# Decoder layer: cross-attention queries and keys projected turned, float32 scores on 32-row strips in pairs of heads

## The reference, cut to what matters

```python
x = _layernorm(x + _L0_attn_ref(x, ...))            # self attention, 3 branches, 16 heads of 96
x = _layernorm(x + _L0_xattn_ref(x, ctx_1024, ctx_1024, mask, ...))
x = _layernorm(x + _L0_ffn_ref(x, ...))             # 8 experts, all computed, 1024 hidden

def _L0_xattn_ref(q, k, v, attention_mask, Wq, bq, Wk, bk, Wv, bv, Wo, bo):   # 16 heads of 16
    qm = _split_heads(q @ Wq.T + bq)
    km = _split_heads(k @ Wk.T + bk)
    vm = _split_heads(v @ Wv.T + bv)
    scores = jnp.einsum('bnlh,bnph->bnlp', qm, km) / np.sqrt(HEAD_DIM)
    scores = jnp.where(mask, scores, MASK_FILL)
    attn = jax.nn.softmax(scores, axis=-1)
    out = jnp.einsum('bnlp,bnph->bnlh', attn, vm)
    return out.transpose(0, 2, 1, 3).reshape(B, L, D_MODEL) @ Wo.T + bo
```

## Time and profile before

| | |
|---|---|
| median of three runs | 2076.5 us (2073.02 to 2076.63) |
| profiled execution | 2072.21 us, span 2070.5 us |
| granted TensorE clock, mean | 0.946 |
| PE busy | 1851.2 us, 89% of the span |
| first row's front and early heads | 0 to about 130 us |
| seven steady rows, one period each | 153.7 us |
| expert part | from about 1290 us to the end |

### The profile page before, as it was taken

The page is one execution under the profiler, slowest core; times in us unless marked ns, Lnnn a source line. Parts: engine busy times, 40 slices in busy tenths (PEclk is TensorE's granted clock), DMA queues, the critical chain, the costliest instruction groups (busy, mean ns, idle before and its releaser), DMA issues. The chain is left out here.

```text
span 2070.5 us, 34799 instructions
## 1 busy us (share of the span) xinstructions
PE 1851.2 (89%) x11880; PEld 1424.9 (69%) x11880; DVE 1244.5 (60%) x4100; ACT 959.6 (46%) x2907; POOL 1039.5 (50%) x1451
## 2 busy tenths in 40 slices
PE   7898898898898898898888875699999999999998
PEld 4565565565565665665665653489999999999997
DVE  4567667667667667667767654563453436445434
ACT  1555755755755756756755754132222212222221
POOL 2453553553553643543643633275665647665553
PEclk9898998998998998998998997699999999999999
DMA  5000000000000000000000000301011010101001
GB/s 157 6 7 1 11 7 6 6 7 2 11 7 6 6 7 6 6 7 6 7 7 1 7 1 25 104 1 41 1 41 41 1 41 1 41 1 41 1 1 41
DMA packets 28656, 37.35 MB, mean 18 GB/s; under 512 B 7160, under 2 KB 23040, under 8 KB 28480
## 3 DMA queue, kind: packets, MB, share of 16 engines
q1 hardware_dynamic: 28480, 35.13, 5.2%
HBM read 30.93 MB, written 4.19 MB: 17 GB/s over the span
## 5 line engine op out<-in xcount | busy, mean ns | idle before, releaser
L1790 POOL TENSOR_TENSOR h_lo<-h_sb,h_hi 128x512 fp32r<-128x512 f32 x256 | 361.1, 1436 | 170.8 <-DVE h_hi L1968 170.8
L1836 ACT ACTIVATE h_sb<-ps_H,b_now 128x512 f32<-128x512 f32 x256 | 176.7, 690 | 532.4 <-PE ps_H L1994 508.3
L548 POOL TENSOR_TENSOR pr<-pr,rden 128x128 f32<-128x128 f32 (+2 forms) x768 | 307.9, 435 | 153.5 <-DVE rden L1039 153.5
L743 ACT ACTIVATE pr<-sm,nmx 128x128 f32<-128x128 f32 (+2 forms) x768 | 311.8, 412 | 34.8 <-DVE nmx L1058 34.5
L1968 DVE CAST h_hi<-h_sb 128x512 fp32r<-128x512 f32 x256 | 234.0, 928 | 144.0 <-ACT h_sb L1836 143.9
L583 POOL TENSOR_TENSOR pr<-pr,rden 128x256 f32<-128x256 f32 x256 | 151.8, 614 | 297.4 <-DVE rden L1039 296.9
L1994 PE MATMUL ps_Y<-w_hi,h_lo 128*128 128x256 f32 x1024 | 289.8, 283 | 0.0
L1994 PE MATMUL ps_Y<-w_lo,h_hi 128*128 128x256 f32 x1024 | 289.8, 283 | 0.0
L1994 PE MATMUL ps_Y<-w_hi,h_hi 128*128 128x256 f32 x1024 | 289.6, 283 | 0.0
L1050 DVE CUSTOM_DVE_ANT_0 sm<-ps_S,cmask 128x128 f32<-128x128 f32 (+2 forms) x768 | 193.3, 309 | 79.7 <-PE ps_S L1259 47.0
L1950 DVE SCALAR_TENSOR_TENSOR x<-ps_Y,route_now,x 128x256 f32<-128x256 f32 x128 | 61.5, 483 | 238.4 <-PE ps_Y L1994 238.4
(11 more groups left out here) (249 smaller groups left out, 3585.0 us busy)
## 6 DMA issues: line engine op xcount, KB each, us to landing
w_raw<-in_W SPq DMA_DIRECT2D x16, 1024.0 KB, 7.5
xin<-in_x SPq DMA_DIRECT2D x8, 256.0 KB, 2.6
cin<-in_ctx SPq DMA_DIRECT2D x8, 256.0 KB, 2.5
x_rows<-x SPq DMA_DIRECT2D x8, 256.0 KB, 2.1
x<-x_rows SPq DMA_DIRECT2D x4, 512.0 KB, 5.9
out<-x SPq DMA_DIRECT2D x4, 512.0 KB, 3.0
w_kw<-in_wink SPq DMA_DIRECT2D x2, 768.0 KB, 6.7
w_ks<-in_selk SPq DMA_DIRECT2D x2, 768.0 KB, 9.7
```

The lines of the kernel that those rows point to most:

```text
L548: last = pool.tensor_tensor(p_, p_, rden[:, h % 2, n:n + 1].to_broadcast([P, width]), ALU.mult)
L743: last = act.activation(pr[:, h % PR_SLOTS, a:a + width], sm[:, h % 2, a:a + width], ACT.Exp, bias=nmx[:, h % 2, n:n + 1], scale=ATT_SCALE ...
L1790: pool.tensor_tensor(h_lo[:, s % 2, ht, :], h_sb[:, ht % 4, :], h_hi[:, s % 2, ht, :].bitcast(F32), ALU.subtract).then_inc(lo_sb.sem, 1)
L1836: ins = act.activation(h_sb[:, ht % 4, :], pst[plan.bank(f)][:, :], ACT.Relu, bias=b1c[:, s // NCH, ht:ht + 1])
```

## The change

Queries and keys are projected *turned* (weights stationary, tokens moving), so channels stand on the partitions. The weight columns are put into an order in which 32 partitions hold two heads, h and h+4. Keys are kept as they are; queries exist twice (`qx[:, a]`), each with the other head's 16 partitions set to zero through `scale=parity`. A head's scores are two float32 matmuls on a strip of 32 rows; two heads h, h+1 lie on different strips and are issued in turn, as a pair, on every second head. There are no bfloat16 parts and no turning of them. The sums of two heads lie in one strip of `ox`: two groups instead of four, and the output projection contracts over 256 rows instead of 512. Main steps in `cross` ahead of the first head fall from 7 to 4 on every engine, DVE, ACT and POOL yield 4 times in their self heads as PE does, and `BREATHERS` becomes (5, 13).

```diff
-BREATHERS = (5, 9, 13)
+BREATHERS = (5, 13)
@@ DVE, cross
-                dve.tensor_copy(split[:, :, 0, :], grouped(lin32)).then_inc(c.step(), 1)
...
-                split_turn("kxT", kxT, 0, 0)
...
+                dve.tensor_copy(mrowf[:, :], mrow[:, :]).then_inc(c.step(), 1)
...
+                for b in range(NC):
+                    ins = dve.scalar_tensor_tensor(kx[:, b, :], ps("kx")[:, T * b:T * b + T], bqk[:, 1, b:b + 1],
+                                                   mrowf[:, :], ALU.add, ALU.mult)
@@ ACT, cross
-                act.copy(split[:, :, 3:6, :], split[:, :, 0:3, :])
...
+                for b in range(NC):
+                    for a in range(2):
+                        ins = act.activation(qx[:, a, b, :], ps("qx")[:, T * b:T * b + T], ACT.Identity,
+                                             bias=bq2[:, a, b:b + 1], scale=parity[:, a:a + 1])
+                        ins.then_inc(qx_sb.sem, 1)
@@ ACT, DVE: heads
-                    if k >= NH - 1:
+                    if k >= NH:
                         yield
@@ PE, cross
-                def scores_x(h):
-                    f = ("sx", h)
-                    pe.wait_ge(plan.free_sem(f), plan.before(f, i))
+                def scores_x(h0):
+                    pe.wait_ge(qx_sb.sem, qx_sb.at(i, h0 // 4 + 1))
+                    for h in (h0, h0 + 1):
+                        pe.wait_ge(plan.free_sem(("sx", h)), plan.before(("sx", h), i))
+                    b, a = h0 // 8, h0 // 4 % 2
                     for q in range(NT):
-                        last = mm(ps(f)[:, T * q:T * q + T], qxT[:, h, P * q:P * q + P], kxT[:, h, :])
-                    last.then_inc(plan.full_sem(f), 1)
+                        for h in (h0, h0 + 1):
+                            strip = slice(HD * (h % 4), HD * (h % 4) + HD)
+                            last = mm(ps(("sx", h))[:, T * q:T * q + T], qx[strip, a, b, P * q:P * q + P],
+                                      kx[strip, b, :])
...
                 for h in range(NH + 4):
-                    if h < NH:
+                    if h < NH and h % 2 == 0:
                         scores_x(h)
```

More of the change, by code:

```diff
@@ L185, in block_plan @@
         plan.add(("pxT", h), "T0")
-    for g in range(4):
+    for g in range(2):
         plan.add(("ox", g), "O")
@@ L573, in cross @@
                 pool.tensor_tensor(x1[:, :, :], x1[:, :, :],
-                                   rows[:, 3:4, :].to_broadcast([P, NT, C]), ALU.add
+                                   rows[:, 1:2, :].to_broadcast([P, NT, C]), ALU.add
                                    ).then_inc(x1b_sb.sem, 1)
@@ L585, in normalise_x @@
                     last.then_inc(prob_sb.sem, 1)
-                for _ in range(3, 7):
-                    yield
+                yield
                 for h in range(NH + 3):
@@ L1140, in cross @@
-                dve.wait_ge(plan.free_sem("kx"), plan.after("kx", i))
-                for t in range(NT):
-                    dve.tensor_scalar(lin32[:, t, :], lin32[:, t, :], mf[:, t:t + 1], None, ALU.mult
-                                      ).then_inc(c.step(), 1)
-                dve.wait_ge(c.sem, c.value())
-                yield
-                dve.tensor_copy(split[:, :, 0, :], grouped(lin32)).then_inc(c.step(), 1)
-                dve.wait_ge(c.sem, c.value())
-                dve.tensor_tensor(grouped(rem), grouped(lin32), split[:, :, 0, :], ALU.subtract).then_inc(c.step(), 1)
@@ L1543, in linear, with turned_linear @@
                     last.then_inc(plan.full_sem(name), 1)
+                def turned_linear(name, src, wt):
+                    pe.wait_ge(plan.free_sem(name), plan.before(name, i))
+                    for b in range(NC):
+                        for c in range(NC):
+                            last = mm(ps(name)[:, T * b:T * b + T], wt[:, c, P * b:P * b + P], src[:, c, :],
+                                      c == 0, c == NC - 1)
+                    last.then_inc(plan.full_sem(name), 1)
                 pe.wait_ge(plan.free_sem("ctxT"), plan.after("ctxT", i))
-                linear("kx", cT, wx_k)
+                turned_linear("kx", cT, wx_k)
                 linear("vx", cT, wx_v)
@@ L2103, in heads @@
         return x.reshape(x.shape[0], NH, parts, HD).transpose(0, 2, 1, 3).reshape(x.shape[0], parts, HW)
+    turned = np.array([XD * (8 * b + 4 * a + j) + d for b in range(NC) for j in range(4) for a in range(2)
+                       for d in range(XD)])
     f = 1.0 / np.float32(10000.0) ** (np.arange(0, RP, 2, dtype=np.float32) / np.float32(RP))
```

199 lines of the change are left out of this document (64 added, 135 removed).

## The result

The changed kernel takes 2256.4 us (median of four runs, 2251.2 to 2257.3) against 2076.6 us: 8.8% slower, ratio 1.0878, 95% interval 1.0859 to 1.0897. Forecast were 2132 us, with a range of 2050 to 2175. The sign was right; more than two thirds of the loss was not foreseen.

The account below looks back on a forecast made before the run. PE, the fullest engine, and its waits were taken as the bound. Seven steady rows at 9.5 - 1.7 + 2 = +9.8 us gave +69, the last row -12: 2072.2 became 2129, 2133 as median, stated as 2132 us; range 2050 to 2175.

Parts of the forecast that it names:

- PE's work: PE in a steady row: pairs at 0.95 us, some 1 us less work; bounds -1.9 and +5.1 us.
- The serial rival: Cross scores: row strips do not overlap, a pair costs 1.73 us plus the change of shape, 2187 us; chance 0.08.
- Waits ahead of the heads: PE before the first pair: new waits of 4.7 us for DVE and 1.4 us for ACT.
- Waits in the heads: PE in the cross heads: 24 us of waits to the next row's first step, where before they were 8.2 us.
- the choice of the tokens: DVE at stage 11: the choice lasts 5.95 us and delays the next pair, so PE waits 3.9 us.
- The clock: PE's clock loss in a steady row: 2 us more, bounds 0 and 8.
- the rival: PE may stay at 1.2 GHz for most of the cross heads: 8 us a row, 2174 us; chance 0.12.
- the window of 71 us: Stretch of a steady row's cross heads as laid out, with 24 us of PE waits in it.
- The order: Front stages beside the same main step on all engines: a steady row's layout ends at 700.0 against 690.55, +9.5 us.
- The rival in which the order does not matter: Heads: ACT and DVE run ahead, waits stay at 8.2 us; row -1.2 us, kernel 2056 us; chance 0.22.
- the 4.7 us wait: PE's key product ahead of the heads waits for DVE's residual, sums of squares and first rotary pair.
- The last row: No front beside it: 14.1 us won before the heads, 5 lost in them, 2.8 won in output projection; together -12 us.

Follow-up runs that it names:

- e7: The changed kernel with its paired cross scores taken over all 128 rows, summing over the heads that share them: 2223 us.
- e10: The changed kernel with ACT, DVE and POOL staggered as before, single heads, queries masked by POOL over all 128 rows: 1995.4 us.
- e3: The changed kernel with ACT, DVE and POOL staggered against PE by one yield, as in the kernel before: 2027.9 us.
- e14: The changed kernel with the stagger given back to ACT and DVE, POOL left as changed: 2002.8 us.
- e17: The changed kernel with ACT and DVE staggered, POOL as changed, POOL-masked queries over all 128 rows, heads in pairs: 2032.5 us.
- e8: The changed kernel with all three engines staggered, single heads over all 128 rows, summing over heads that share them: 1988.3 us.
- e5: The changed kernel with the stagger given back to DVE alone: 2191.9 us.
- e6: The changed kernel with the stagger given back to ACT alone: 2138.3 us.
- e9: The changed kernel with all three engines staggered and one head of scores per step on its 32-row strip: 2089.1 us.
- e13: The changed kernel with all three engines staggered, single heads over 64 rows, summing over heads that share them: 2069.5 us.
- e12: The changed kernel, no stagger, with single heads over all 128 rows, summing over heads that share them: 2326.8 us.
- e4: The kernel before, bfloat16 scores kept, with the changed kernel's yields and placing of the gate's exponential and reciprocal: 2389.7 us.

## Why the prediction was wrong

**PE's work: right.** +0.4 us a row on the mean, -0.8 in the row shown, against -1. Pairs cost 1.06 us at full clock; I had 0.95. The serial rival is out: with two strips a record costs 0.13 us, alone 0.216; the pairs over 128 rows (e7) show the serial price, 1.72. The Trainium skill (TensorEngine Tiling (Array Packing), When to Use Tiling) advises row tiling where 64 rows or fewer are contracted. For the pairs' own time the trace agrees. For the kernel it depends on the order: with three engines staggered full rows with zeros are faster (e10, 1995 us, against e3, 2028), with two the strips are (e14, 2003, against e17, 2033).

**Waits ahead of the heads: right.** 4.23 us for 4.7, 1.16 for 1.4; from the turned context to the first pair 21.9 us for 20.0, the rest clock (3.00 us for a key product of 1.7).

**Waits in the heads: right in place, near in size.** ACT's `rot`, `v_sb` and `qT_sb`: 2.13, 2.32, 1.97 for 2.4 each. DVE: 1.96, 1.47, 1.91 for 1.2 to 2.1. Only the largest, 3.9 us behind the choice of the tokens, is 0.80; PE came late to it at half speed, and in e7, where the clock is higher, it is 3.20. All idle time of a row grew by 11.6 us on the mean; what is left of the forecast row without work and clock is 8.8.

**The clock: wrong, and this is the step that failed.** "I add 2 us; bounds 0 and 8." It was 12.9 us a row on the mean of six and 18.9 in the row shown. The seven stretches from one self projection to the next lost 179 us together, near 26 each, where I had 9.8. I had scaled the loss of the kernel before, taken from a row that loses 5.4 us where the mean of six is 7.4, and given the rival 8 us a row as if that were the end of what the clock can take. Two things stood against it. First, the window of 71 us that I had laid out held some 47 us of busy time, and at the lower level all of that can double; 8 was no bound from rows. Second, I weighed the strips only for their overlap. That the scores change from bfloat16 matmuls of all 128 rows to float32 matmuls of 32 was in the diff; what such matmuls do to the clock was in no row of before, and an unknown of that kind needs a bound of its own. The runs give both: e3 takes back 12.4 us a row of the clock's loss by order alone, e7 9.0 by the rows of the array alone (20.3 to 11.4, mean of six), against some 6 us of work more.

**The order** was named as the step that decides, and it was, but at a price that was too low. e3 shows that the new scores are a gain of 2.1% (2028 us) with the stagger kept, e14 one of 3.3%. The rival in which the order does not matter had 2056 us, and 2024 without the 4.7 us wait. Its row without that wait, 147.7 us, is the one that e3 has (147.1 on the mean of six). Its condition, that ACT and DVE get ahead by themselves, is false: they need the stagger, and without it the kernel takes 228 us more.

**The last row:** -12 us forecast, none came. Ahead of the heads it won 12.3 us (22.7 from the turned context to the first scores before, 10.4 after) for 14.1: ACT's four copies hold the bank for 2.27 us, where I had only the first quarter of the queries in the way. In the heads it lost 14.9 us (34.6 before, 49.5 after) for 5: the clock, 0.55 for 0.75. e14, with the same pairs and 0.79, has 40.4 us in that place, close to the 39.6 of the forecast; e8 at 1.00 has 33.5.

**What remains open:** why 32 or 64 rows lower the clock, and whether it is the rows, or float32 with few rows; no bfloat16 strips were run. Why the same pairs with the same waits stand at 0.55 in one last row and at 0.79 in another. How far waits alone lower the clock is not tied to one wait: e5, e6 and e14 do not add.

## What to carry to other kernels

When generators or loops are woven by count, a dropped `yield` is a change of the schedule of the whole kernel: keep the stagger of the engines while you change the arithmetic, and change it in a run of its own. Here it was worth 228 us, the arithmetic 44 the other way.

Price the clock as a term with its own upper bound: busy time in the stretch, doubled. It can be larger than the waits that go with it.

Small row strips of the array may be paid for by the clock of everything beside them. Where the operand can be masked by an idle engine, full rows with zeros can be faster: 1995 against 2089 us for single heads, at the same number of columns. Measure it in the order that will stay: pairs on strips came to 2003 us in their best one, and beat full rows there.

## What the runs showed of the hardware

- Two float32 heads on different 32-row strips, their records alternating, take 1.06 us for eight records; over 128 rows 1.72, both heads on one strip 1.92.
- In the last row's cross heads, with float32 scores of 32 or 64 rows, the granted clock is 0.52 while PE hardly idles; with 128 rows it is 1.00 in the same place (single heads: e9, e13, e8; e10 with zeros in 112 of the rows). Pairs of heads on two strips of 32 rows have 0.51 to 0.79 there (e3, the changed kernel, e6, e14).
- With full rows and many waits it falls too, to 0.76 in the cross heads of e12, where PE idles for 24 of 100 us:

```profile
361.40:461.90 100.50, 76.57 (x305) 46.69 (x304) 39.08 (x139) 32.65 (x95) 26.14 (x38) 0.76 0.01 3
```

- The bfloat16 scores of 128 rows in the changed order (e4) stand at 0.72 to 0.76 in these heads, so that the kernel before is no safer from a wrong order than the changed one: it loses 318 us by it.
